# A token mixer's value matmuls in quarters of the array, with the softmax denominators from half sums added on GpSimd and VectorE

## The reference, cut to what matters

```python
q, k, v = jnp.split(qkv, 3, axis=1)          # qkv: (128, 96, 512)
scale = 1.0 / np.sqrt(np.sqrt(ch))           # ch = 32
weight = jnp.einsum('bct,bcs->bts', q * scale, k * scale)
weight = jax.nn.softmax(weight.astype(jnp.float32), axis=-1).astype(weight.dtype)
return jnp.einsum('bts,bcs->bct', weight, v)
```

## Time and profile before

| | |
|---|---|
| time, median of 3 executions | 2330.69 us (2326.32 to 2330.86) |
| the profiled execution | 2332.05 us, its span 2330.2 us |
| TensorE busy | 2230.4 us, 96% of the span |
| VectorE, ScalarE, GpSimd busy | 1630.9, 1523.8, 1080.4 us |
| granted TensorE clock, mean | 0.990 |

### The profile page before, as it was taken

One profiled execution on the slowest core, in us unless ns is written; L12 is line 12 of the kernel. 1 busy time (PEld: TensorE's weight loads), 2 busy tenths in 40 slices (PEclk: granted clock), 3 DMA queues, 4 the chain that ended last, 5 costly groups with the idle time before them and its releaser, 6 DMA issues. The chain is left out here.

```text
span 2330.2 us, 41583 instructions
## 1 busy us (share of the span) xinstructions
PE 2230.4 (96%) x13316; PEld 1135.3 (49%) x13316; DVE 1630.9 (70%) x2893; ACT 1523.8 (65%) x2430; POOL 1080.4 (46%) x1045
## 2 busy tenths in 40 slices
PE   7999999998999998899999999999998999999997
PEld 2333333334666665444444444666664444444443
DVE  6666666674788989666667633666666787788775
ACT  4666666666788787445556423766675777777775
POOL 1322223236877778322324401444454566666654
PEclk9999999998999999999999999999999999999999
DMA  5555555441334221312222212222221011111111
GB/s 141 138 138 131 130 135 133 128 129 50 102 129 129 69 74 63 103 48 80 75 88 95 75 50 68 78 81 81 81 82 42 23 50 51 41 50 41 42 37 63
DMA packets 144303, 194.97 MB, mean 84 GB/s; under 512 B 32773, under 2 KB 76261, under 8 KB 144154
## 3 DMA queue, kind: packets, MB, share of 16 engines
q1 hardware_dynamic: 115642, 154.79, 22.1%
q10 hardware_dynamic: 28512, 38.28, 5.9%
HBM read 125.10 MB, written 42.21 MB: 72 GB/s over the span
## 5 line engine op out<-in xcount | busy, mean ns | idle before, releaser
L341 DVE TENSOR_REDUCE tm_negmax<-tm_s 128x1 f32<-128x512 f32 x512 | 323.6, 679 | 159.3 <-PE tm_s L384 158.9
L2222 PE MATMUL f_bank<-f_xs,gu 128*128 128x512 f16 x1408 | 417.0, 379 | 1.6 <-ACT f_firstg L2048 1.1
L303 ACT ACTIVATE tm_prob<-tm_s 128x1024 f32<-128x1024 f32 x256 | 257.6, 1023 | 132.4 <-PE tm_s L404 126.6
L2250 PE MATMUL f_bank<-dn,f_ghi 128*128 128x512 f16 x704 | 265.5, 379 | 1.9 <-DVE f_glo L2157 1.9
L421 PE MATMUL tm_o<-tm_prob,tm_vt 128*64 128x512 f32 x1024 | 255.7, 620 | 0.0
L384 PE MATMUL tm_s<-tm_qk 96*128 96x512 f16 x512 | 200.6, 394 | 27.2 <-DMA tm_qk<-tm_xs 15.6
L2012 POOL TENSOR_TENSOR f_firstg<-f_firstg,f_secondg 128x512 f32<-128x512 f32 x88 | 152.3, 1730 | 153.1 <-DVE f_secondg L2141 153.1
L2222 PEld LDWEIGHTS f_bank<-f_xs,gu 128*128 128x128 f16 x1408 | 135.9, 98 | 162.8 <-ACT f_firstg L2048 1.5
L264 POOL TENSOR_TENSOR tm_hn<-tm_nd,tm_rows 128x1024 f32<-128x1024 f32 x32 | 75.2, 2351 | 289.1 <-DMA tm_rows<-rden 289.1
L404 PE MATMUL tm_s<-tm_qk 98*128 98x512 f16 x512 | 194.6, 384 | 0.3 <-DMA tm_qk<-tm_mrow 0.2
L987 PE MATMUL a_bankB<-a_wo,a_yThi 128*128 128x512 f16 x512 | 155.5, 386 | 0.0
(11 more groups left out here) (193 smaller groups left out, 5648.1 us busy)
## 6 DMA issues: line engine op xcount, KB each, us to landing
tm_qk<-tm_xs SPq DMA_DIRECT2D x384, 64.0 KB, 2.1
tm_xqk<-in_qk ACTq DMA_DIRECT2D x32, 512.0 KB, 4.6
a_hin<-h SPq DMA_DIRECT2D x64, 256.0 KB, 2.6
a_hres<-h SPq DMA_DIRECT2D x64, 256.0 KB, 3.0
h<-a_hout SPq DMA_DIRECT2D x64, 256.0 KB, 2.6
f_hin<-h SPq DMA_DIRECT2D x64, 256.0 KB, 2.9
f_hres<-h SPq DMA_DIRECT2D x64, 256.0 KB, 2.9
tm_vt<-in_vt ACTq DMA_DIRECT2D x32, 256.0 KB, 3.1
```

The lines of the kernel that those rows point to most:

```text
L303: nc.scalar.activation(prob[b][:, 2 * h:2 * h + 2, :], s2[:, i % 2, :, :], ACT.Exp, scale=SCALE).then_inc(exp_done, 1)
L341: nc.vector.tensor_reduce(negmax[u][:, m:m + 1], s1[:, p % BANKS, :], AX.X, ALU.max, negate=True).then_inc(s1_read, 1)
L2222: last = nc.tensor.matmul(bank_of(m, i)[:, :], (gate, up)[which][:, j, m * P:(m + 1) * P], xs[g % 2][:, x, j, :], start=x == 0, stop=x == 1)
L2250: last = nc.tensor.matmul(pz[i][:, :], gparts[x][:, (MT * g + m) % RING, i * P:(i + 1) * P], down[w][:, m, :], start=m == 0 and c % 3 == 0 ...
```

## The change

The stationary operand of the values loses its columns of ones and has 32 columns. All four sequences of a tile lie side by side in the four quarters of the array, one position block j (128 positions) at a time: `sum_values` runs at slot 14, and for the rest at slots 0, 2 and 4 of the next step. For the denominators, the exponentials of blocks 0 and 1 are added to those of blocks 2 and 3 (`added`, 128x1024 float32 a sequence), by GpSimd for three sequences (`add`) and by VectorE for the fourth (`add_last`). Two more groups, `sum_probs` at slots 8 and 10 of the next step, multiply these by ones, into bank 2 of `s1`. The A results therefore turn in two banks from slot 5 to slot 11, by the table `BANK`. ScalarE copies values and sums separately (`copy_values`, `copy_sums`). Buffers and DMAs of the normalisation have half their size, and it runs in place; the inverses move one step later. The diff, cut:

```diff
+    BANK = (1, 2, 0, 1, 2, 0, 1, 0, 1, 0, 1, 0, 1, 2, 0, 1, 2, 0)
+    SUMS_BANK, FIRST_BEHIND_SUMS = 2, 13
...
+    ones = sb("tm_ones", [P, C], F32)
     negmax = [sb(f"tm_negmax{i}", [P, SLOTS], F32) for i in range(2)]
     mrow = [sb(f"tm_mrow{i}", [HALF, 2, P], F16) for i in range(2)]
     prob = [sb(f"tm_prob{i}", [P, NT, T], F32) for i in range(B)]
...
+    added = [sb(f"tm_added{i}", [P, 2, T], F32) for i in range(B)]
     s1 = ps("tm_s1", [P, BANKS, T], F32)
...
-    VALUES_AT = {7: 0, 11: 1, 15: 2, 3: 3}
+    VALUES_AT = {14: (0, 0), 0: (1, 1), 2: (1, 2), 4: (1, 3)}
+    SUMS_AT = {8: 0, 10: 1}
+    BEFORE = [max(q for q in range(p - USES, p) if BANK[q % USES] == BANK[p]) for p in range(USES)]
 
...
             stack(n + 1, 1 - u, 2)
+            stack(n + 1, 1 - u, 3)
+            inverses(n - 2, u, k - 1)
+            maxima(n, u, 1)
             inverse_rows(n - 2, u, k - 1)
-            stack(n + 1, 1 - u, 3)
-            maxima(n, u, 1)
-            denominators(n - 1, 1 - u)
             stack(n + 2, u, 0)
             stack(n + 2, u, 1)
             maxima(n + 1, 1 - u, 0)
-            inverses(n - 1, 1 - u, k + u - 1)
+            denominators(n - 1, 1 - u)
         return step, store
 
     def rows_ready(sp, t):
...
+        def add(t, b):
+
+            if inside(t, TILES):
+                wait(pool, exp_done, 8 * t + (3, 4, 7)[b])
+                wait(pool, sums_done, t)
+                pool.tensor_tensor(added[b][:, :, :], prob[b][:, 0:2, :], prob[b][:, 2:4, :], ALU.add)\
+                    .then_inc(added_done, 1)
 
         def step(k, u):
             n = 2 * k + u
-            normalise(n - 2, u, k - 1)
+            add(n - 1, 2)
             x_lo(n + 3, 1 - u)
-        return step
+            if not isinstance(n, int) or n < TILES:
+                normalise(n - 2, u, k - 1)
+            add(n, 0)
+            add(n, 1)
+        return step, normalise
 
     def scalar(act):
...
                 wait(act, s2_ready, 8 * t + i + 1)
-                if i % 2 == 0:
-                    wait(act, pv_done, 4 * (t - 1) + i // 2 + 1)
+                if i == 5:
+                    wait(act, last_added, t)
+                elif i % 4 < 2:
+                    wait(act, added_done, 3 * (t - 1) + b + 1)
+                if i in (0, 2):
+                    wait(act, pv_done, 4 * (t - 1) + i + 2)
                 nc.scalar.activation(prob[b][:, 2 * h:2 * h + 2, :], s2[:, i % 2, :, :], ACT.Exp,
                                      scale=SCALE).then_inc(exp_done, 1)
...
+        def copy_values(t, u, half):
+
+            if inside(t, TILES):
+                wait(act, pv_done, 4 * t + 4)
+                wait(act, stored[u], 16 * half)
+                nc.scalar.copy(nd[u][:, 0, :], o[:, :]).then_inc(values_out, 1)
+
+        def copy_sums(t, u):
+
+            if inside(t, TILES):
+                wait(act, sums_done, t + 1)
+                nc.scalar.copy(nd[u][:, 1, :], sums_bank(t)).then_inc(sums_out, 1)
 
...
         def step(k, u):
             n = 2 * k + u
             for i in range(8):
                 exps(n, i)
-                if i == 1:
-                    sums_out(n - 1, 1 - u, 1)
                 if i == 2:
+                    copy_values(n - 1, 1 - u, k + u - 1)
                     load_values(n + 1, 1 - u)
                 if i == 3:
                     x_hi(n + 3, 1 - u, k + 1 + u)
                 if i == 4:
+                    copy_sums(n - 1, 1 - u)
                     load(n + 4, u)
-                if i == 5:
-                    sums_out(n, u, 0)
...
+        def add_last(t):
+
+            if inside(t, TILES):
+                wait(dve, exp_done, 8 * t + 8)
+                wait(dve, sums_done, t)
+                nc.vector.tensor_tensor(added[B - 1][:, :, :], prob[B - 1][:, 0:2, :], prob[B - 1][:, 2:4, :],
+                                        ALU.add).then_inc(last_added, 1)
...
-                if g == 12:
-                    inverse_sums(n - 1, 1 - u, k + u - 1)
-        return step
+                if g == 1:
+                    inverse_sums(n - 2, u, k - 1)
+                if g == 3:
+                    add_last(n - 1)
...
                 wait(pe, s1_read, freed(t, place(m)))
-                nc.tensor.matmul(s1[:, place(m) % BANKS, :], qk[u][0:KS, 0, b, i * P:(i + 1) * P],
+                if place(m) == FIRST_BEHIND_SUMS:
+                    wait(pe, sums_out, t - 1)
+                nc.tensor.matmul(s1[:, BANK[place(m)], :], qk[u][0:KS, 0, b, i * P:(i + 1) * P],
                                  qk[u][0:KS, 1, b, :], start=True, stop=True).then_inc(s1_ready, 1)
...
-        def sum_values(t, u, half, r):
-
-            if inside(t, TILES):
-                pair, h = r // 2, r % 2
-                if r == 0:
+        def sum_values(t, u, half, j):
+
+            if inside(t, TILES):
+                if j == 0:
                     wait(pe, v_in[u], 16 * (half + 1))
-                if h == 0:
-                    wait(pe, nd_done, 2 * t + pair)
-                wait(pe, exp_done, 8 * t + 2 * r + 2)
-                for j in (2 * h, 2 * h + 1):
-                    for q in range(2):
-                        b = 2 * pair + q
-                        last = nc.tensor.matmul(o[2 * C * q:2 * C * (q + 1), :], vt[u][:, j, :, b],
-                                                prob[b][:, j, :], start=j == 0, stop=j == NT - 1)
+                    wait(pe, values_out, t)
+                if j % 2 == 0:
+                    wait(pe, exp_done, 8 * t + 6 + j)
+                for b in range(B):
+                    last = nc.tensor.matmul(o[C * b:C * (b + 1), :], vt[u][:, j, :, b], prob[b][:, j, :],
+                                            start=j == 0, stop=j == NT - 1)
                 last.then_inc(pv_done, 1)
+
+        def sum_probs(t, j):
+
+            if inside(t, TILES):
+                if j == 0:
+                    wait(pe, added_done, 3 * (t + 1))
+                    wait(pe, last_added, t + 1)
+                    if isinstance(t, int) and t == TILES - 1:
+                        wait(pe, exp_done, 8 * t + 8)
+                    elif isinstance(t, int) and t == TILES - 2:
+                        wait(pe, s1_read, use(t + 1, 16) + 1)
+                        wait(pe, sums_out, t)
+                    else:
+                        wait(pe, s1_read, use(t + 2, 4) + 1)
+                out = sums_bank(t)
+                for b in range(B):
+                    last = nc.tensor.matmul(out[C * b:C * (b + 1), :], ones[:, :], added[b][:, j, :],
+                                            start=j == 0, stop=j == 1)
+                if j == 1:
+                    last.then_inc(sums_done, 1)
...
                 scores_for_max(n + ahead, (u + ahead) % 2, k + (u + ahead) // 2, m)
                 scores(n, u, g)
-                r = VALUES_AT.get(g)
-                if r == 3:
-                    sum_values(n - 1, 1 - u, k + u - 1, r)
-                elif r is not None:
-                    sum_values(n, u, k, r)
-        return step
+                behind, j = VALUES_AT.get(g, (0, None))
+                if j is not None:
+                    sum_values(n - behind, (u + behind) % 2, k - behind + (u and behind), j)
...
         run(mix, 31, 31)
-        run(step, -3, -2)
+        run(step, -3, -3)
+        run(mix, 32, 32)
+        run(step, -2, -2)
         prepare(WO)
-        run(step, -1, 0)
-        run(mix, 32, 32)
-        run(step, 1, 1)
-        run(mix, 33, 33)
-        run(step, 2, 27)
+        run(step, -1, 2)
+        normalise_mixed(30, 0, 15)
+        run(step, 3, 4)
+        normalise_mixed(31, 1, 15)
+        run(step, 5, 27)
```

More of the change, by code:

```diff
@@ L99, in token_mixer @@
     rden = [sb(f"tm_rden{i}", [P, E], F32) for i in range(2)]
-    rows = [sb(f"tm_rows{i}", [P, 2, T], F32) for i in range(2)]
-    hn = [sb(f"tm_hn{i}", [P, 2, T], F32) for i in range(2)]
+    rows = [sb(f"tm_rows{i}", [P, T], F32) for i in range(2)]
+    added = [sb(f"tm_added{i}", [P, 2, T], F32) for i in range(B)]
     s1 = ps("tm_s1", [P, BANKS, T], F32)
@@ L261, in normalise @@
             if inside(t, TILES):
-                wait(pool, rows_in[u], 32 * (half + 1))
-                wait(pool, stored[u], 32 * half)
-                pool.tensor_tensor(hn[u][:, :, :], nd[u][:, :, :], rows[u][:, :, :], ALU.mult)\
+                wait(pool, rows_in[u], 16 * (half + 1))
+                pool.tensor_tensor(nd[u][:, 0, :], nd[u][:, 0, :], rows[u][:, :], ALU.mult)\
                     .then_inc(norm_done, 1)
+        def add(t, b):
[4 more added lines that the diff above has]
+                    .then_inc(added_done, 1)
         def step(k, u):
             n = 2 * k + u
-            normalise(n - 2, u, k - 1)
+            add(n - 1, 2)
             x_lo(n + 3, 1 - u)
-        return step
+            if not isinstance(n, int) or n < TILES:
[3 more added lines that the diff above has]
+        return step, normalise
     def scalar(act):
@@ L323, in step @@
```

(34 more changed lines are left out.)

82 lines of the change are left out of this document (44 added, 38 removed).

## The result

The changed kernel takes 2357.89 us (median of 4 runs, 2357.19 to 2359.64), the kernel before 2330.78 on the same chip: ratio 1.0122, 95% interval 1.0104 to 1.0139. It is 27 us slower; the forecast was 15.5 faster. The profiled execution has a span of 2355.4 us, before 2330.2, so 25.2 us have to be found.

A forecast was written before the change was run, and what follows sets the result against it. The prediction took TensorE as the bound, VectorE near behind. 31 steps going from 16.06 to 15.49 us take 17.7 off, the ends put 2.2 on: -15.5 us, a forecast median of 2315 us, range 2299 to 2343.

The forecast's parts named there:

- The group at 1.16: TensorE matmul groups in quarters: each costs 1.16 us instead of 2.02, six costing 6.96 instead of 8.08.
- First half 8.18: Walk from the transposes of slot 3 to those of slot 11: 8.18 us, about 1.1 of it waiting for VectorE.
- the forecast wait at slot 7: TensorE's maximum score matmul of slot 7 needs slot 5's bank: reached at 3.0 us, starts at 3.95.
- Second half: From the transposes of slot 11 to those of slot 3: 7.31 us, the maxima's DMA hidden by 0.35.
- forecast gain of 0.57 a step: Loop step of one tile: from 16.06 us before to 15.49 after the change.
- The ring at 15.44: Loop chain from slot 7 through GpSimd's three adds and the held add_last back to slot 7, just under the step.
- the walk: Step followed slot by slot through both halves: 8.18 + 7.31 = 15.49 us.
- rival (1): GpSimd's three adds and the held add_last close the step harder: slower, +15 to +84 us; chance 0.18.
- Smaller edits: Copies, DMAs, inverses, memsets: SP issues less and is no bound; for later inverses, nothing waits but the store.
- Ends, +2.2: Mixer's last tiles: VectorE held once, about +1.9 us for tile 29, and +0.3 in the last step.
- Rival (3): Near ties (ring, sums' copy, maxima by DMA) slip or group is 1.3: step 15.9 to 16.2, 2326 to 2335 us; chance 0.18.
- the range: Whole kernel's time, 8 in 10: 2299 to 2343 us.

The follow-up runs named there:

- e1: Changed kernel with the 512 KB load of the next queries and keys issued behind exponential 7 instead of exponential 4: 2357.27 us, ratio 1.0110.
- e3: Changed kernel with GpSimd's three additions of a tile at half width, the other half of the sums left out: 2346.27 us, ratio 1.0065.
- e5: Changed kernel with the 512 KB load behind exponential 7 and GpSimd's three additions at half width: 2329.98 us, ratio 1.0008.
- e4: Changed kernel with SyncE's attention loads of tiles 6 and 7 ahead of the mixer's last inverses and rows: 2350.01 us, ratio 1.0088.
- e9: e4 plus tile 31's store behind the attention's step 4 loads and GpSimd's last normalisation one attention step earlier: 2343.31 us, ratio 1.0056.
- e7: Changed kernel with the 512 KB load behind exponential 7 and add_last at slot 6 instead of slot 3: 2341.98 us, ratio 1.0049.
- e10: e7 with e9, and the 1 MB load of attention output weights in tile 28 behind exponential 7: 2326.53 us, ratio 0.9987.

## Why the prediction was wrong, point by point

- **The group at 1.16.** Right: 1.03 from group to next A; counted as the forecast did, from the B ahead and less that B's 0.22, it is 1.12. By the figure for column tiles in the Trainium skill, "TensorE: Matmul & The Clock Gate", section "Part 3: Packing small matmuls", the prediction's estimate was 1.38; the trace does not bear it out.
- **First half 8.18.** Right: 7.99 to 8.09, with the forecast wait at slot 7.
- **Second half, "B of 0 needs the maxima by DMA ... so 3.54, hidden by 0.35".** This is the step that failed. I took 2.63 from the first tile, where next to nothing else was in flight (2 GB/s from 23.7 to 25.6 us). In the loop the landing is at 4.2 to 5.6 and is the last to arrive: from T of slot 11 to T of slot 3 it takes 8.17 in the mean instead of 7.31, and these 0.86 are more than the whole forecast gain of 0.57 a step. The trace of before had it. There T is at 308.12, and these rows stand behind it:

```profile
308.21 0.40 ACTq L277 DMA_DIRECT2D tm_xqk<-in_qk  x1
...
310.13 1.44 SPq L198 DMA_DIRECT2D tm_qk<-tm_mrow  x2
...
315.05 0.38 PE L404 MATMUL tm_s<-tm_qk 98*128 98x512 f16 x1
```

  The landing is 5.51 behind T, 3.5 behind the first issue, and B of slot 0 came at 6.93. It was hidden by 1.4, and the change, which pulls B of slot 0 forward by 3.0, uncovers it. An issue at 1.09, 3.5 to the landing and 0.12 to the matmul put B of slot 0 at 4.7, 0.8 later than forecast, and the step at 16.3: no gain. e1 shows the cause: with the load moved behind, the maxima land at 3.6 and this half takes 7.30.
- **The ring at 15.44, 0.05 short of the walk.** In the changed kernel it does not bind (e3). Once the load is out of the way it does (e1, e5): add_last is held by GpSimd's third add, at the place that rival (1) named, and the first half costs 0.67 a step more in the mean. A margin of 0.05 was none: adds start at uneven times, and a hold of 0.9 cost 1.0 us with the clock at 1.00 and 2.5 where the clock fell, for which the forecast had no price. In the changed kernel the DMA masked all this.
- **Smaller edits: "SP is no bound", "nothing waits but the store".** Wrong at the hand-over: 7.3 us between projections 0 and 8, of which 6.3 are the attention's load queued behind a store that waits for GpSimd (e4, e9).
- **Ends, +2.2.** Too small: +7.2 from tile 28 to the projections. The forecast had one held add, +1.9; there are two (2.26 and 2.54 instead of 1.20), one with a fall of the clock behind it (0.71 from 505 to 510 us) and one without (1.00 from 520 to 530), and all of tiles 28 to 30 costs 2.3. The larger part, 4.9 against a forecast of 0.3, is the last tile, where the wait for `a_rstd` was left out: VectorE's queue also holds the attention's first steps, and these wait for GpSimd. This is read from the trace; no run takes that wait away. e3, with GpSimd's adds at half width, takes back 5.5 of the 7.2.
- **Rival (3)**, near ties that slip, named the maxima by DMA among three and gave a step up to 16.2. That is what the loop did; it had 0.18. Its 2326 to 2335 leave out the +2.2 of the ends (with them, 2328 to 2337), and neither it nor the range held the losses of the last tiles and of the queues at the hand-over.

Not settled: why in tile 6 in particular SyncE's queue is late and the landing with it (e7 and e10 have such a wait at the other T, in tile 6 and in tile 4), and the 3.4 us behind projections 8.

## What to carry to other kernels

When a change brings a consumer forward, list every producer of it that was hidden, and size each from a row of the same loop, with the same transfers in flight, and never from the first tile. A queue that issues in order is a chain like an engine: whatever a moved instruction waits for, all DMAs behind it wait too, also those of the next stage. And take two near ties in one loop as one unit: here taking out one alone gave 0.21 or 0.02 us a step, both together 0.85. A large load moved out of one step's way can stand in the next one's, as the 1 MB load did.
